# Paired row halves in a projection, reordered first loads of an attention, and one gather of slot numbers with early expert weights

## What is computed

```python
x = x + conv_attn(group_norm(x))            # 12 heads of 16, with relative positions
t = t + attn(layer_norm(t))                 # 12 heads of 16, without
t = t + moe(layer_norm(t))                  # 16 experts, top 1

# conv_attn, for 12 heads and 8 images
attn  = einsum('bhqd,bhkd->bhqk', q * scale, k)
rel_h = einsum('bnhwd,hkd->bnhwk', rq, Rh)  # rq is q as (b, head, 32, 32, 16)
rel_w = einsum('bnhwd,wkd->bnhwk', rq, Rw)
attn  = softmax(attn + rel_h[..., :, None] + rel_w[..., None, :])

# moe: each token goes to the expert with the largest logit
h = gelu(t @ W1[e].T + b1[e]); y = h @ W2[e].T + b2[e]
```

## Time and profile before

| what | value |
|---|---|
| median of 3 runs | 3566.92 us (3561.04 to 3567.52) |
| profiled execution | 3567.99 us, its span 3566.4 us |
| mean granted clock of PE | 0.877 of 2.4 GHz |
| busy: PE / DVE / ACT / POOL | 2999.4 / 2460.8 / 1857.8 / 1035.9 us |
| first projection | 0 to 388.05 us |
| start of attention, PE idle | 372 to 435.02 us |
| route and start of experts, to the first gather | 2997.4 to 3287.80 us |

### The profile page before, as it was taken

How to read it: one execution, slowest core, us unless ns; L and a number is a source line. 1 busy time by engine, 2 the same in 40 slices (tenths; PEclk the granted TensorE clock), 3 DMA queues, 4 the chain that set the end, 5 groups by cost and what they waited for, 6 DMA issues and landing times. The chain is left out here.

```text
span 3566.4 us, 65082 instructions
## 1 busy us (share of the span) xinstructions
PE 2999.4 (84%) x17813; PEld 1218.8 (34%) x17814; DVE 2460.8 (69%) x4482; ACT 1857.8 (52%) x2383; POOL 1035.9 (29%) x1684
## 2 busy tenths in 40 slices
PE   4999299999999999987886999999999995430777
PEld 3778122222222222225661222222222221430666
DVE  3443199898899988943546999999999992430211
ACT  2333047666666666672340777777777774100332
POOL 0000223333333333313212333333333321242555
PEclk9666579999999999997895999999999998555877
DMA  4655625554544445524754222222222224703211
GB/s 92 176 169 156 135 55 105 107 103 98 100 98 100 100 99 99 105 55 112 199 139 96 66 67 66 66 66 65 66 66 66 66 55 111 112 18 61 53 49 35
DMA packets 303082, 325.71 MB, mean 91 GB/s; under 512 B 148784, under 2 KB 235645, under 8 KB 298377
## 3 DMA queue, kind: packets, MB, share of 16 engines
q0 software_dynamic: 76544, 192.13, 24.3%
q1 hardware_dynamic: 190346, 119.79, 13.2%
q10 hardware_dynamic: 36096, 12.60, 2.2%
HBM read 217.71 MB, written 109.19 MB: 92 GB/s over the span
## 5 line engine op out<-in xcount | busy, mean ns | idle before, releaser
L487 DVE TENSOR_REDUCE a_halfmax<-a_psR 128x1 f32<-128x512 f32 x3072 | 1963.6, 686 | 213.9 <-PE a_psR L342 195.7
L442 ACT ACTIVATE a_probs<-a_psS 128x1024 f32<-128x1024 f32 x1536 | 1488.3, 1021 | 814.8 <-PE a_psS L360 810.7
L360 PE MATMUL a_psS<-a_qrows,a_krows 121*128 121x512 f16 (+1 forms) x3072 | 805.4, 384 | 55.4 <-DMA a_qrows<-relh 51.2
L371 PE MATMUL a_psO<-a_probs,a_v 128*32 128x512 f32 x6144 | 829.3, 612 | 1.2 <-ACT a_probs L442 1.2
L342 PE MATMUL a_psR<-a_kmax,a_qmax 64*128 64x512 f16 x3072 | 685.7, 400 | 99.5 <-DMA a_krows<-in_onehot 62.8
L342 PEld LDWEIGHTS a_psR<-a_kmax,a_qmax 64*128 64x128 f16 x3072 | 161.2, 93 | 1092.5 <-DVE a_halfmax L487 951.6
L360 PEld LDWEIGHTS a_psS<-a_qrows,a_krows 121*128 121x128 f16 (+1 forms) x3072 | 242.6, 98 | 427.9 <-issue 158.7
L203 POOL DMA_DIRECT2D a_qmax<-qk x240 | 122.2, 509 | 700.7 <-PE a_psO L371 601.7
L187 POOL DMA_DIRECT2D a_qrows<-qk x240 | 123.6, 515 | 276.5 <-PE a_psO L371 257.2
L811 PE MATMUL p_psQ<-p_xnT,p_wqk 96*128 96x512 f32 x384 | 184.7, 645 | 14.3 <-DVE p_xnT L964 12.2
L371 PEld LDWEIGHTS a_psO<-a_probs,a_v 128*32 128x32 f32 x6144 | 121.5, 108 | 184.4 <-issue 177.0
(11 more groups left out here) (157 smaller groups left out, 2261.8 us busy)
## 6 DMA issues: line engine op xcount, KB each, us to landing
a_qrows<-qk POOLq DMA_DIRECT2D x240, 128.0 KB, 3.8
qk<-p_half SPq DMA_DIRECT2D x96, 256.0 KB, 3.3
v<-p_v SPq DMA_DIRECT2D x48, 512.0 KB, 6.2
a_qrows<-rel POOLq DMA_DIRECT2D x96, 256.0 KB, 4.5
a_v<-v POOLq DMA_DIRECT2D x96, 256.0 KB, 3.1
a_krows<-qk POOLq DMA_DIRECT2D x168, 128.0 KB, 3.7
a_qmax<-qk POOLq DMA_DIRECT2D x288, 64.0 KB, 2.3
a_kmax<-qk POOLq DMA_DIRECT2D x240, 64.0 KB, 2.3
```

The source lines that it names most:

```text
L360: mm = nc.tensor.matmul(psS[:, (2 * n + j) % 4, :], K[buf][:, h, keys], A[buf][kt % NA][:, h, queries], start=True, stop=True)
L371: mm = nc.tensor.matmul(psO[32 * h:32 * h + 32, :], V[buf][:, kt, h, :], PT[:, blk % 2, h, :], start=(kt == 0), stop=(kt == KT - 1))
L442: nc.scalar.activation(PT[:, blk % 2, 2 * pair:2 * pair + 2, :], psS[:, b0:b0 + 2, :], ACT.Exp, scale=scale).then_inc(exped, 1)
L487: nc.vector.tensor_reduce(mx[:, unit, half:half + 1], psR[:, slot, :], AX.X, ALU.max)\
```

## The change

**In the first projection** the banks are taken in pairs: a list `BANKS` names group, `hw`, `x0` and first partition of each bank. For `hw` = 0 and then 1, banks of group 0 (partitions 0-63) and group 1 (64-127) alternate; then group 2 follows with `hw` = 0 on partitions 0-63 and `hw` = 1 on 64-127. For the latter a copy `Q2` of the queries of group 2 is made on the upper partitions by SP, two transfers of 256 KB a round. Within a pair PE alternates between the two banks with every matmul. Number and shape of the matmuls stay. The stores of groups 0 and 1 now wait for two thirds of the round's banks, those of group 2 for all.

**At the start of an attention** POOL issues `load(0)` ahead of `load_maxima(1)`. SP loads the constants of both `KM` first, on semaphores of their own, then waits for `loadedm[0]`, and only then loads those of `K`. PE waits for the constants of `KM[0]` and for `loadedm[0]` before the first maxima, for `KM[1]` and `loadedm[1]` before those of the second unit, and for the rest before the first scores.

**In route and experts** the weights of the experts are loaded by SP in route, after the third link of the first round's normalisation. The list `TILES` in DRAM and the 80 small loads of slot numbers are gone: at the end of route POOL gathers the slot numbers of all 80 tiles by one indirect transfer, DVE makes them f32, PE transposes them and DVE writes them as the tile `IXA` in SBUF that experts reads. The experts of the tiles stay in SBUF as well.

```diff
             for blk in range(BLK):
                 load_maxima(0, 0, blk)
             for blk in range(BLK):
+                load(0, 0, blk)
+            for blk in range(BLK):
                 load_maxima(1, 1, blk)
-            for blk in range(BLK):
-                load(0, 0, blk)
...
+            for i in range(2 if rel else 0):
+                for r in range(2):
+                    at = 64 * r + HD
+                    sp.dma_start(KM[i][at:at + WI, :, :], every(onehot_dram[HI:REL, :], 2)).then_inc(const_km[i], 16)
...
+            sp.wait_ge(loadedm[0], 16 * NLOADM)
...
             pe.wait_ge(const_done, 2)
-            pe.wait_ge(const_dma, CONSTS)
+            if rel:
+                pe.wait_ge(const_km[0], 16 * 6)
             pe.wait_ge(loadedm[0], 16 * NLOADM)
             for n, j in enumerate(FIRST):
                 if n == HALVES + 1:
                     pe.wait_ge(loadedm[1], 16 * NLOADM)
+                    if rel:
+                        pe.wait_ge(const_km[1], 16 * 6)
                 job(n, j, 0, first_slot(n), n + 1, 0, 0, 0)
+            pe.wait_ge(const_dma, CONSTS)
...
+            XS = range(0, HI, RX)
+            BANKS = ([(g, hw, x0, 64 * g) for hw in range(2) for x0 in XS for g in range(2)] +
+                     [(2, hw, x0, 64 * hw) for x0 in XS for hw in range(2)])
...
                     store_half(j, m, half)
+                    if first and m == 1:
+                        sp.dma_start(Q2[64:P, half, :], HL[half][0:64, 1, :]).then_inc(q2, 16)
...
-                        sp.wait_ge(rlo, j * NR + (NR // NG) * (g + 1) + 4)
+                        sp.wait_ge(rlo, j * NR + (2 * NR // NG, NR)[g // 2] + 4)
...
+                    for n in range(0, NR, 2):
+                        if n == 0:
+                            pe.wait_ge(hi, j * NCH + 1)
+                            pe.wait_ge(lo, j * NCH + 2)
+                        if n == 2 * NR // NG:
+                            pe.wait_ge(q2, j * 32 + 32)
+                            pe.wait_ge(hi, j * NCH + 2)
+                            pe.wait_ge(lo, j * NCH + 3)
+                        pe.wait_ge(rlo, j * NR + (n + 2))
+                        for x in range(RX):
+                            for i, (part, of) in enumerate(((0, 0), (0, 1), (1, 0))):
+                                for side in range(2):
+                                    g, hw, x0, r = BANKS[n + side]
+                                    o = psR[:, (n + side) % 4, :].rearrange("p (b x y) -> p b x y", b=2, x=RX)
...
+                    for n, (g, hw, x0, _) in enumerate(BANKS):
+                        act.wait_ge(rps, j * NR + (n + 1))
...
+            sp.wait_ge(nm, 3 + NM0)
+            for w, (wt, bias) in zip(W, WEIGHTS):
+                sp.dma_start(w[0:CC], wt.rearrange("(c p) e n -> p c e n", p=CC)).then_inc(wl, 16)
+                sp.dma_start(w[CC:CC + 1, 1], bias.rearrange("(o e) n -> o e n", o=1)).then_inc(wl, 16)
...
-            sp.wait_ge(fin, 18)
-            sp.dma_start(TILES, TR[:, :]).then_inc(out, 16)
-            sp.wait_ge(out, 16)
...
+            pool.wait_ge(fin, 15)
+            pool.indirect_dma_start(SL[:, :], None, SLOTS.rearrange("(r p) o -> r (p o)", p=P),
+                                    bass.IndirectOffsetOnAxis(ap=ROW[0:NTILE, 0:1], axis=0)).then_inc(slots, 16)
...
+            pe.wait_ge(fin, 19)
+            nc.tensor.transpose(psK[:, 0:NTILE], SLF[:, :], ident[0:NTILE, 0:NTILE]).then_inc(fin, 1)
...
+            dve.wait_ge(slots, 16)
+            step(19, nc.vector.tensor_copy(SLF[:, :], SL[:, :]))
+            dve.wait_ge(fin, 20)
+            step(21, nc.vector.tensor_copy(IXA[:, :], psK[:, 0:NTILE]))
...
-            sp.wait_ge(tl, 16)
-            nc.sync.sem_inc(ixa[1], 1)
-            load_slots(sp, 0, UN // 2, ixa[0])
-            load_slots(sp, UN, NTILE, ixa[1])
...
-            pool.wait_ge(ixa[0], 16 * UN)
```

More of the change, by code:

```diff
@@ L88, in attention @@
         const_dma = sem("const_dma")
+        const_km = [sem(f"const_km{i}") for i in range(2)]
         loaded = [sem(f"loaded{i}") for i in range(2)]
@@ new lines, in round_of @@
+                    for n in range(0, NR, 2):
[12 more added lines that the diff above has]
+                                    o = psR[:, (n + side) % 4, :].rearrange("p (b x y) -> p b x y", b=2, x=RX)
+                                    if g < 2:
+                                        q = HL[of][r:r + 64, 0, :]
+                                    elif r == 0:
+                                        q = HL[of][0:64, 1, :]
+                                    else:
+                                        q = Q2[64:P, of, :]
+                                    q = q.rearrange("p (b h w) -> p b h w", b=2, h=HI)
+                                    xx = x0 + x
+                                    table = RTS[part][r:r + 64, hw, HI - 1 - xx:2 * HI - 1 - xx, :]
+                                    mm = nc.tensor.matmul(o[:, :, x, :], table.rearrange("p k h -> p (k h)"),
+                                                          q[:, :, xx, :] if hw == 0 else q[:, :, :, xx],
+                                                          start=(i == 0), stop=(i == 2))
+                                    if x == RX - 1 and i == 2:
+                                        mm.then_inc(rps, 1)
@@ L1027, in round_of @@
                 else:
-                    n = 0
-                    for g in range(NG):
-                        for hw in range(2):
-                            for x0 in range(0, HI, RX):
-                                if n % 4 == 3 and n // 4 < PAIR // 512:
-                                    at = 512 * (n // 4)
-                                    low_half(j, NCH - 1, slice(at, at + 512))
-                                dve.wait_ge(rhi, j * NR + (n + 1))
-                                dst, src = rel_views(g, 1, hw, x0, n % 4)
-                                high, _ = rel_views(g, 0, hw, x0, n % 4)
-                                for b in range(2):
-                                    a = nc.vector.tensor_tensor(dst[b], src[b], high[b], ALU.subtract)
-                                a.then_inc(rlo, 1)
-                                n += 1
+                    for n, (g, hw, x0, _) in enumerate(BANKS):
+                        if n % 4 == 3 and n // 4 < PAIR // 512:
+                            at = 512 * (n // 4)
+                            low_half(j, NCH - 1, slice(at, at + 512))
+                        dve.wait_ge(rhi, j * NR + (n + 1))
+                        dst, src = rel_views(g, 1, hw, x0, n % 4)
+                        high, _ = rel_views(g, 0, hw, x0, n % 4)
+                        for b in range(2):
+                            a = nc.vector.tensor_tensor(dst[b], src[b], high[b], ALU.subtract)
+                        a.then_inc(rlo, 1)
                 if ahead:
@@ L1061, with route @@
 EMPTY = 1 << 20
-def route(nc, name, X2, ON, WG, BG, X3, SLOTS, TILES):
+def route(nc, name, X2, ON, WG, BG, X3, SLOTS, W, WEIGHTS, wl, TR, IXA):
     NT = PAIR // P
@@ L1140, in route @@
         fin = sem("fin")
-        out = sem("out")
+        slots = sem("slots")
         rsq = sem("rsq")
@@ L1263, in _ @@
             pe.wait_ge(fin, 16)
-            nc.tensor.transpose(psC[0:2, 0:P], TL[:, :], ident[:, :]).then_inc(fin, 1)
+            nc.tensor.transpose(psC[0:1, 0:P], TL[:, :], ident[:, :]).then_inc(fin, 1)
+            pe.wait_ge(fin, 19)
+            nc.tensor.transpose(psK[:, 0:NTILE], SLF[:, :], ident[0:NTILE, 0:NTILE]).then_inc(fin, 1)
         @block.scalar
@@ L1440, in experts @@
         psY = ps("psY", [P, 2, 512])
-        tl = sem("tl")
-        wl = sem("wl")
         made = sem("made")
-        ixa = [sem(f"ixa{i}") for i in range(2)]
         ix = sem("ix")
@@ L1638, in hybrid_block @@
     attention(nc, "a2", False, 1.0 / float(np.sqrt(C)), QK2, None, None, VN2, O2, a["onehot"])
-    route(nc, "r", X2, O2, a["wg"], a["bg"], X3, SLOTS, TILES)
-    experts(nc, "e", X3, SLOTS, TILES, a["w1"], a["b1"], a["w2"], a["b2"], out)
+    with ExitStack() as ctx:
+        W = [ctx.enter_context(nc.sbuf_tensor(f"f_w{i}", [CC + 1, 2, E_N, C], F32)) for i in (1, 2)]
+        TR = ctx.enter_context(nc.sbuf_tensor("f_tileExpert", [1, P], I32))
+        IXA = ctx.enter_context(nc.sbuf_tensor("f_slotsAll", [P, NTILE], I32))
+        wl = ctx.enter_context(nc.semaphore("f_wl"))
+        route(nc, "r", X2, O2, a["wg"], a["bg"], X3, SLOTS, W, ((a["w1"], a["b1"]), (a["w2"], a["b2"])), wl, TR, IXA)
+        experts(nc, "e", X3, W, wl, TR, IXA, out)
 DRAM_KIND = "Internal"
```

91 lines of the change are left out of this document (24 added, 67 removed).

## The result

The kernel after takes 3466.93 us (median of 4 runs, 3465.52 to 3469.05) against 3563.98 of the kernel before on the same chip: a ratio of 0.973, 95% interval 0.9713 to 0.9746. The forecast was 3460 us and 107 saved; 97 were saved between the medians. Stages follow each other behind barriers, so I take both traces apart at the barriers first. They come from one profiled execution of each kernel, and these two lie 102.5 us apart (3567.99 and 3465.52), so some 5 us of the changes in the table are scatter of single executions.

A forecast was written before the change was run, and what follows sets the result against it. PE was taken to bound the first projection's rounds, 83 us each. First projection 46, attention's start 32, and route and experts 29 sum to 107 us off a median of 3566.9: 3460 us, range 3436 to 3505.

The forecast's parts named there:

- own two signs of being wrong: First projection: wrong if strided pairs pace above 0.15 us, or if the store tail reaches into the next round's halves.
- Halves at once, strided pair 0.110 us: Relative products: matmuls on both row halves run at once, so a pair with `hw` = 1 costs 0.110 us, not 0.220.
- The sum by ring and DVE: Relative products: twelve pairs of banks, walked through bank fills and DVE's differences, need 30.4 us a round, not 44.1.
- Plain pair 0.058 us: Relative products: a pair with `hw` = 0 costs at least 0.058 us, so a pair of banks fills in 1.4 us.
- The estimate of 0.100 us a plain pair at the low clock: Relative products with `hw` = 0: some 60 cycles a matmul make a pair some 0.100 us, taking some 4 us from the gain.
- Gap between rounds: First projection: the 3.31 us gap to the next round grows by 0.8 us, three times, losing 2.4 us.
- The stores' tail: First projection: the stage ends 23 us after PE's last matmul, where it was 16, losing 7 us once.
- The last half of k: First projection: it has landed some 17 us after the round's end, and ACT writes the next half after 21.
- Attention's start: First attention: PE's first job starts at 403 us against 435.05, saving 32 us (30 to 36).
- Route and experts: First gather at 3255 us against 3287.8 gains 33; early weights in route lose 4 (0 to 16); together 29.
- Clock: Rival: denser pairs keep the clock up, next q and k gain some 3 us a round, 3451 us; with good covers 0.04.
- The drain on a change of half: Rival in the relative products: each change of half empties the array, 400 us more, 3905 us; chance 0.03.

The follow-up runs named there:

- e10: Kernel after, but relative products with `hw` = 1 read neighbouring elements, making half the relative tables wrong: 3442.87 us, ratio 0.9665.
- e2: Kernel after, but SP stores groups 0 and 1 by table, `hw` = 0 after bank 8, last half of k then `hw` = 1 after bank 16: 3396.69 us, 0.9657.
- after_again: Kernel after, unchanged, run again on chip 11: 3418.96 us, ratio 0.9716 to the kernel before.
- e4: Kernel after, but the weights are loaded at the start of experts, as in the kernel before: 3427.68 us, ratio 0.9741.
- e3: Kernel after, but SP loads the experts' weights behind route's rounds, after the last store of x3: 3409.43 us, ratio 0.9678.
- e8: Kernel after with both the stores of e2 and the weights of e3: 3392.59 us, ratio 0.9636.
- e1: Kernel after, but within a pair PE fills one bank before the other instead of alternating with every matmul: 3435.05 us, ratio 0.977.
- e9: Kernel after with 40 loads of slot numbers by SP at the start of experts, into a tile nothing reads: 3418.12 us, ratio 0.9713.

## Why the prediction was right, point by point

The total lies 7 us from the forecast and within its range, and the three gains come from the places named. That it is so near is in part luck, for terms were off both ways: the relative products gave 6 us more than said and the stores behind them took some 12 more; in route the early weights cost more than said and the new work less. And of its own two signs of being wrong one occurred: the stores' tail did reach into the next round's halves, for 3.7 us.

- **Halves at once, strided pair 0.110 us**: right, 0.108 to 0.11 and 2.65 us a pair of banks. The sum by ring and DVE gave 30.4 us a round, measured 28.2 to 30.2.
- **Plain pair 0.058 us**: the step "a pair costs at least twice the 0.029 us in which a weight load and a matmul have been issued" was wrong; a pair takes 0.031 us at the high clock, at which these banks start a round, and 0.053 to 0.057 at the low one (e10). The relative products saved 61 us and not 55. The estimate of 0.100 us a plain pair at the low clock, worked out from the 60 cycles a matmul of the Trainium skill (page TensorEngine Tiling (Array Packing), section Instruction Overhead), added up the cycles of both halves. e10's 0.053 to 0.057 is about half, near the 0.049 of a single matmul at that clock: if there is such an overhead, both halves have it at once. The runs don't contradict the page's figure for one matmul.
- **Gap between rounds**: the forecast 0.8 us more, measured 0.6 (3.87 before the first weight load, 3.31 in the earlier trace rows). Right.
- **The stores' tail**: mechanism right, size off. I took 28 us from the first issue at 1.09 us each and 3 us to land; the 26 transfers took 1.26 each, and the last one landed 5.8 us after its issue, 29.5 behind the last matmul and not 23. These are 6.5 us of the miss.
- **The last half of k**: "some 17 us after the round's end, and writes after 21" left 4 us of cover. It was gone in the third round: landed 24 us after the round's end and not 17, 3.7 us of wait and a low clock, some 6 us in all. I averaged the transfers over a round of 69 us (48 of 69), but the order of one queue decides, not the average. e2 takes the wait away and the tail back to 17.1 with the order alone.
- **Attention's start**: 32 forecast, 34 measured (13.0 after the barrier, forecast 15). `load_maxima(1)` and krows were hidden, as said.
- **Route and experts**: 33 less 4 forecast, 29; measured 27.3 on the first chip and 27.6 on that of after_again (5.9 more, 33.5 less). The sum is right, its terms in route are not. The first gather goes out 4.8 us into the stage, as said. From the last scatter's end to the barrier it takes 22.6 to 26.2 us with the new slot numbers (ten traces) and 20.7 to 22.2 without (four): some 2 us of new work, forecast 4. The early weights cost more than the 4 us that I took "between 0 and the whole 16": the second root is 107.4 to 114.4 us into route in the seven traces with early weights, 109.2 in the mean, and 99.5 to 105.1 in the seven others, 101.8 in the mean, so 7 us. And the wait is not the one named. I had the late loads of x slow the scatters that POOL waits for. In all seven traces with early weights it is the other way round: POOL waits for DVE, and DVE gets the third round's x 98 to 105 us into the stage, after 37 to 45 us of waiting. In the other seven the root waits for the scatters, and DVE for nothing. By e4 the early loads buy 16 us of experts, and by e3 and e8 they can be had without the delay.
- **Clock**: not up. 0.57 and 0.66 over the relative products, and q and k began at a high clock as before.
- **The drain on a change of half**: not there. 2304 changes cost nothing that a trace shows; e1, which changes 24 times a round, is the slower one. All these matmuls have one form, 64 rows by 128 columns, and change only the half.

What stays open: whether the second root's delay differs between chips. It is 9.3 us in the result's pair (114.4 against 105.1), 6.6 on chip 8, 4.1 to 8.8 on chip 11 and 6.5 to 9.7 on chip 15, and single executions without it scatter by 5.6 us. Open too is whether the tiles gain some 4 us where they are slow (275.4, 277.0 and 274.3 us with the old route, 270.1, 271.7 and 271.2 with the new one); e9, which kept slot loads, ran where they are fast.

## What to carry to other kernels

When a stage gets faster, its stores don't: list the transfers of a queue in the order in which their data are ready, and ask for each who waits behind it. Here the same stores cost 17 to 19 us more in one order than in another, and plain reads would have lost half of what they gained to them. Work that can't start before a barrier because one late load was issued after an early one that nobody needs yet is the cheapest gain of all: 34 us for three moved groups of loads. Bring a bulk load forward to the last place where the DMA engines idle, not to the first: behind the rounds the weights were still in time and cost the roots nothing.

## What was unexpected of the hardware

- Two matmuls of 64 rows and 64 columns on the two row halves start within 0.01 us of each other, and a pair is issued every 0.031 us, hardly slower than a single one before (0.029). With moving elements that lie 32 apart (f16) a half takes 0.110 us, beside the other half or alone, and at either level of the clock.
- Even without alternation the halves overlap (e1): a bank of 24 matmuls on one half has its first four beside the last of the bank before, 2.20 us in place of 2.65. By their start times matmuls of the later bank even pass those of the earlier one, 184.89 and 184.99.
- Loads and scatters share a stretch unevenly: with the weights ahead of it DVE waited 37 to 45 us for the third round's x, while the scatters of the same stretch landed no later than before (97 to 99 us into route against 100 to 103, in the traces of chips 8 and 11).
- 80 tiles of indirect gathers and scatters took 216 to 220 us on chips 8 and 11 (226 in e4) and 250 to 260 on chip 15 and in the result's pair, whose chip has no number on record, with either kernel. That is most of the 45 us between the medians of the kernel before (3517 to 3520, 3562 to 3564).
